# Preparing a state-space scan by batch pair, and moving 19 of its products to GpSimd

## The reference, cut to what matters

```python
x = einsum('bld,ed->bel', ctx, in_proj_w); x = silu(conv1d(x, conv_w) + conv_b)     # u, 256 channels
dt_low, Bm, Cm = split(einsum('bdl,ed->bel', x, x_proj_w), [8, 24])                  # 8 + 16 + 16 rows
dt = softplus(einsum('brl,dr->bdl', dt_low, dt_proj_w) + dt_proj_b)                  # delta
def step(state, inp):                                                                # 256 time steps
    state = state * exp(dt * A) + (dt * u) * B                                       # 16 states a channel
    return state, einsum('bdn,bn->bd', state, C)
y = (y + D * u) * silu(layernorm(x))                                                 # then x = x + y
```

## Time and profile before

| what | value |
|---|---|
| median of 3 runs | 987.07 us (983.51 to 987.46) |
| the profiled execution's own time | 985.21 us |
| its span | 983.4 us |
| mean granted clock of PE | 0.912 |
| busy PE, DVE, ACT, POOL | 82%, 75%, 47%, 25% |

### The profile page before, as it was taken

How to read it: one execution, slowest core, us unless ns; L and a number is a source line. 1 busy time by engine, 2 the same in 40 slices (tenths; PEclk the granted TensorE clock), 3 DMA queues, 4 the chain that set the end, 5 groups by cost and what they waited for, 6 DMA issues and landing times.

```text
span 983.4 us, 11811 instructions
## 1 busy us (share of the span) xinstructions
PE 806.8 (82%) x3952; PEld 577.3 (59%) x3952; DVE 741.3 (75%) x1080; ACT 459.3 (47%) x951; POOL 243.4 (25%) x162
## 2 busy tenths in 40 slices
PE   6822549997788996698998987988984789999997
PEld 3312435555533473466665665656763579999996
DVE  4599899999987897789899788869956744434443
ACT  1422445563114302467666656646773434544542
POOL 1072200000223012101011021111002447666663
PEclk9765658998899999899999999999997799999999
DMA  4222133221502022011111111011200034433431
GB/s 158 91 95 84 44 107 107 107 86 65 203 2 90 22 86 86 3 46 40 63 44 44 44 44 43 23 43 43 88 1 0 1 128 156 149 139 129 157 129 43
DMA packets 24176, 74.60 MB, mean 76 GB/s; under 512 B 3088, under 2 KB 5664, under 8 KB 23744
## 3 DMA queue, kind: packets, MB, share of 16 engines
q1 hardware_dynamic: 23776, 71.51, 20.7%
q10 hardware_dynamic: 352, 2.49, 0.8%
HBM read 72.55 MB, written 1.44 MB: 75 GB/s over the span
## 4 chain that ended last, share of the span: by engine, by line
PE 46%; DVE 30%; issue 11%; ACT 8%; POOL 2%; DMA 0%; POOLq 0%; DVEq 0%; SPq 0%; ACTq 0%
DVE hS L846 10%; PE ps L1457 6%; PE ps L1571 6%; PE ps L1572 6%; PE ps L1573 6%; DVE hS L838 4%; PE ps L1420 4%; PE ps L1536 3%; PE ps L1437 2%; PE ps L1524 2%; PE ps L1222 2%; PE ps L1230 2%; DVE arena L1097 2%; ACT dA L509 1%; PE ps L1515 1%
## 5 line engine op out<-in xcount | busy, mean ns | idle before, releaser
L846 DVE TENSOR_TENSOR_SCAN hS<-dA,hS 128x1024 f32<-128x1024 f32 x64 | 157.8, 2465 | 21.7 <-ACT dA L509 20.5
L1230 PE MATMUL ps<-ident,hS 128*128 128x128 f32 x512 | 75.8, 299 | 49.6 <-DVE hS L849 49.4
L1203 DVE SCALAR_TENSOR_TENSOR arena<-ps,arena 128x1024 f32<-128x1024 f32 x32 | 39.2, 1225 | 102.0 <-ACT arena L724 93.1
L1230 PEld LDWEIGHTS ps<-ident,hS 128*128 128x128 f32 x512 | 64.2, 154 | 77.7 <-DVE hS L849 59.3
L1457 PE MATMUL ps<-WB,hT 128*128 128x512 f32 x192 | 88.7, 606 | 3.8 <-DVE arena L1078 2.0
L509 ACT ACTIVATE dA<-DEL,negA 128x510 f32<-128x510 f32 x128 | 84.8, 717 | 12.3 <-DVE hS L846 11.8
L423 POOL TENSOR_TENSOR MHl<-arena,MHh 128x1024 fp32r<-128x1024 f32 x34 | 81.7, 2404 | 16.7 <-ACT MHh L727 16.7
L849 DVE TENSOR_TENSOR hS<-hS,BCb 128x1024 f32<-128x1024 f32 x64 | 83.6, 1306 | 2.2
L1571 PE MATMUL ps<-Wh,MHh 128*128 128x256 f32 x272 | 77.8, 286 | 6.0 <-POOL MHl L423 6.0
L409 POOL TENSOR_SCALAR jst<-jst 128x8 f32<-128x8 f32 x20 | 12.3, 613 | 279.6 <-DVE jst L1086 279.6
L838 DVE TENSOR_TENSOR hS<-DU,BCb 128x1024 f32<-128x1024 f32 x64 | 77.8, 1216 | 0.1
(11 more groups left out here) (206 smaller groups left out, 1889.5 us busy)
## 6 DMA issues: line engine op xcount, KB each, us to landing
BCb<-bc_dram SPq DMA_DIRECT2D x64, 512.0 KB, 3.6
arena<-gate_dram SPq DMA_DIRECT2D x32, 512.0 KB, 3.7
WB<-in_we SPq DMA_DIRECT2D x34, 256.0 KB, 2.7
WB<-in_wqkv SPq DMA_DIRECT2D x1, 3072.0 KB, 12.9
WA<-in_wo ACTq DMA_DIRECT2D x1, 2048.0 KB, 7.7
WA<-in_ffn SPq DMA_DIRECT2D x1, 1408.0 KB, 6.5
pkb<-in_pk SPq DMA_DIRECT2D x2, 698.0 KB
X<-in_x SPq DMA_DIRECT2D x1, 1024.0 KB, 7.4
```

The lines of the kernel that those rows point to most:

```text
L846: v.tensor_tensor_scan(f(h), f(a), f(h), 0.0, ALU.mult, ALU.add).then_inc(s["scan_done"], 1)
L1230: last = mm(ps[:, ACC_BANK + j // 2, 256 * (j % 2) + P * d:256 * (j % 2) + P * d + P], src[:, d, P * j:P * j + P], ident[:], start=(first ...
```

## The change

1. The preparation is done for each pair of the batch alone (k = 0, 1 in layer 0, k = 2, 3 in layer 1), with instructions of half the length. In layer 0 pair 0 is prepared first and half steps 0 to 2 run ahead of the rest of pair 1's preparation. Of the preparation, `d_u` moves from DVE to ACT, and for k above 0 so do `u_half`, max(z,0) (a Relu) and the addition of 1.
2. DVE's list in the head is reordered: half steps 3 to 5, then the rotary mean, 6 and 7, then the norm. PE adds half steps 0 to 7 ahead of the attention's transposes (0 to 3 before); ACT copies the projections after the exponentials of half step 2, and makes those of half steps up to 9 before it waits for `rope0_done` (up to 5 before).
3. `POOL_STEPS = range(8, 27)`: for half steps 8 to 26 of the first layer the C product moves to GpSimd, and the B product is written to PSUM banks 4 and 5, from which the scan reads it. The attention's PSUM banks shrink for it: scores have banks 0 and 1 alone, values bank 2, transposes bank 3, and `s0(u)` waits for tanh(u-1).
4. SP loads X ahead of two small tensors, and the second layer's weights after `delta_ready` 2.

```diff
+POOL_STEPS = range(8, 27)
+        def temps(k):
+            if k == 1:
+                two = lambda a: a.rearrange("p (d t) -> p d t", d=DT)
+                return (two(ar(38, 1024)), two(ar(42, 1024)), two(WB[:, 0, 2048:3072]), ar(46, 512)[0:DR + 2 * DS, :])
+            i = k % 2
+            return (ring(hS, 2 * i), ring(hS, 2 * i + 1), ring(dA, 2 + i), ring(dA, i)[0:DR + 2 * DS, 0, :])
@@ GpSimd, behind rope0_done
+            def times_c(g):
+                pool.wait_ge(s["scan_done"], g + 1)
+                pool.wait_ge(ld_bc[g % SB_LOADS], 16 * (g // SB_LOADS + 1))
+                h = ring(hS, g)
+                gp.tensor_tensor(h, h, BCb[g % SB_LOADS][:, 1:2, :].broadcast_to([P, DT, HALF]), ALU.mult).then_inc(s["c_ready"], 1)
+            for g in POOL_STEPS:
+                times_c(g)
@@ ACT
+            def softplus(k):
+                act.wait_ge(s["dtpre_mm"], k + 1)
...
+                for d in range(DT):
+                    sc.activation(DEL[:, d, pair(pr)], ps[:, CONV_BANK[l] + 2 * pr + d, :], ACT.Relu,
+                                  bias=pk[l][:, PK_DB + d:PK_DB + d + 1]).then_inc(s["sp_max"], 1)
+                act.wait_ge(s["sp_exp"], k + 1)
+                sc.activation(one, e, ACT.Identity, bias=1.0).then_inc(s["sp_one"], 1)
...
             neg_a(0)
             for d in range(DT):
                 conv_tanh(0, d)
-            ln_tr_copy(0)
+            conv_tanh(1, 0)
             xdbl_copy(0)
             softplus(0)
             softplus_ln(0)
-            for t in range(NT):
-                act.wait_ge(s["qkv0_mm"], t + 1)
-                sc.copy(Q0[:, t, :], ps[:, 4 + t % 4, 0:NQKV0]).then_inc(s["qkv0_copied"], 1)
+            conv_tanh(1, 1)
+            for d in range(DT):
+                u_half(1, d)
+            ln_tr_copy(0)
...
+            steps_to(0)
+            d_u(0)
+            xdbl_copy(1)
+            steps_to(1)
+            softplus(1)
+            softplus_ln(1)
             steps_to(2)
+            for t in range(NT):
+                act.wait_ge(s["qkv0_mm"], t + 1)
+                sc.copy(Q0[:, t, :], ps[:, 4 + t % 4, 0:NQKV0]).then_inc(s["qkv0_copied"], 1)
@@ DVE
+            def dbu(g):
+                return ps[:, DBU_BANK:DBU_BANK + 2, :] if g in POOL_STEPS else ring(hS, g)
...
-                v.tensor_tensor(ring(hS, g), DU[:, :, pair(pr)], b, ALU.mult).then_inc(s["dbu_ready"], 1)
+                if g in POOL_STEPS:
+                    dve.wait_ge(s["scan_done"], g)
+                    dve.wait_ge(s["qkv0_copied"], NT)
+                v.tensor_tensor(dbu(g), DU[:, :, pair(pr)], b, ALU.mult).then_inc(s["dbu_ready"], 1)
...
-                v.tensor_tensor_scan(f(h), f(a), f(h), 0.0, ALU.mult, ALU.add).then_inc(s["scan_done"], 1)
+                v.tensor_tensor_scan(f(h), f(a), f(dbu(g)), 0.0, ALU.mult, ALU.add).then_inc(s["scan_done"], 1)
+                if g in POOL_STEPS:
+                    return
                 dve.wait_ge(s["scan_done"], g + 1)
+                if g == POOL_STEPS.stop:
+                    dve.wait_ge(s["c_ready"], g)
...
-            for g in range(4, LAYER_STEPS - 4):
+            for g in range(8, LAYER_STEPS - 4):
                 ssm_step(g)
                 for u in range(UNITS0):
                     if AT0_AT[u] == g:
                         at0(u)
@@ PE
+            conv(1, (0,))
+            xdbl(0)
+            dtpre(0)
+            conv(1, (1,))
             pe.wait_ge(ld["ident"], 16)
             ln_tr(0)
-            xdbl(0)
+            xdbl(1)
+            dtpre(1)
             pe.wait_ge(ld["wqkv0"], 16)
-            dtpre(0)
...
-            for g in range(4):
+            for g in range(8):
                 acc(g)
             pe.wait_ge(s["rope0_done"], 1)
...
-                if u >= 2:
-                    pe.wait_ge(s["s0_tanh"], u - 1)
+                if u:
+                    pe.wait_ge(s["s0_tanh"], u)
```

More of the change, by code:

```diff
@@ L263, in build @@
         CONV_BANK = [0, 4]
+        DBU_BANK = 4
         ACC_BANK = 6
@@ L293, in _ @@
                 load_bc(g)
-            sp.wait_ge(s["delta_ready"], 1)
-            sp.wait_ge(s["sp_exp"], 1)
+            for g in range(SB_LOADS, 8):
+                load_bc(g)
+            sp.wait_ge(s["delta_ready"], 2)
+            sp.wait_ge(s["sp_exp"], 2)
             sp.wait_ge(s["nega_exp"], 1)
@@ L302, in _ @@
             sp.dma_start(dsc[:], io["dsc"]).then_inc(ld["ffn"], 16)
-            for g in range(SB_LOADS, LAYER_STEPS):
+            for g in range(8, LAYER_STEPS):
                 load_bc(g)
@@ L600, in _ @@
             neg_a(1)
-            for d in range(DT):
-                conv_tanh(1, d)
+            for k in (2, 3):
+                for d in range(DT):
+                    conv_tanh(k, d)
+                for d in range(DT):
+                    u_half(k, d)
             ln_tr_copy(1)
@@ new lines, in u_calc, with delta_max0 @@
+            def u_calc(k, d, mark=None):
+                l, pr = prep(k)
+                if k == 0:
+                    ch.wait(mark)
+                else:
+                    dve.wait_ge(s["conv_tanh"], DT * k + d + 1)
+                    dve.wait_ge(s["u_half"], DT * (k - 1) + d + 1)
+                v.scalar_tensor_tensor(U[:, d, pair(pr)], DEL[:, d, pair(pr)], 1.0, DU[:, d, pair(pr)], ALU.add,
+                                       ALU.mult).then_inc(s["u_ready"], 1)
+            def delta_max0():
+                for d in range(DT):
+                    dve.wait_ge(s["sp_abs"], d + 1)
+                    ch.step(v.tensor_scalar(DEL[:, d, pair(0)], ps[:, CONV_BANK[0] + d, :], pk[0][:, PK_DB + d:PK_DB + d + 1], 0.0,
+                                            ALU.add, ALU.max))
@@ L898, in _ @@
                 ln_stats(0, hf)
+            for d in range(DT):
+                u_calc(0, d, u_half0(d))
             for hf in both:
                 ln_apply(0, hf)
-            for d in range(DT):
-                u_calc(0, d, u_half(0, d))
-            for hf in both:
-                ln_tr_copy(0, hf)
-            delta_max(0)
+            delta_max0()
             delta_round(0)
@@ L909, in _ @@
             ssm_dbu(0)
-            d_u(0)
+            for hf in both:
+                ln_tr_copy(0, hf)
+            for d in range(DT):
+                u_calc(1, d)
+            ssm_scan(0)
+            ssm_step(1)
+            ssm_step(2)
+            delta_round(1)
+            delta_sum(1)
+            delta_u(1)
             dve.wait_ge(s["qkv0_copied"], NT)
@@ L996, in _ @@
                 ln_tr_copy(1, hf)
-            marks = [u_half(1, d) for d in range(DT)]
-            for d in range(DT):
-                u_calc(1, d, marks[d])
+            for k in (2, 3):
+                for d in range(DT):
+                    u_calc(k, d)
             dve.wait_ge(ld["ffn"], 48)
```

267 lines of the change are left out of this document (149 added, 118 removed).

## The result

The changed kernel takes **992.24 us** (median of 7 runs, 989.90 to 993.62) beside 986.74 us for the kernel before on the same chip (982.50 to 988.82): a ratio of 1.0077, 95% interval 1.0049 to 1.0104. 981.5 us was forecast, with a range to 991. The profiled execution of after took 993.62 us, its span 991.8.

A forecast was written before the change was run, and what follows sets the result against it. DVE was taken to bound the head, with PE almost level (5.08 against 5.14 us) in unit half steps. 985.2 - 2.7 - 1.9 = 980.6, or 982.5 from the median; 981.5 was taken, own range 977 to 987, with rivals 972 to 991.

The forecast's parts named there:

- DVE starts 0.03 us later, GpSimd 0.08 us later, so DVE is first: Half steps without at0: after a scan, DVE's B product gets the port before GpSimd's C product.
- the 3.57: Forecast length in us of a half step without at0, 1.22 + 2.29 + 0.06, against 4.72 before.
- the forecast's own case: The main forecast, no rival coming true: 981.5 us, own range 977 to 987, chance 0.58.
- The mid transpose: Around scan(20) to scan(22): PE's chain from at0(8) to at0(9) stays 8.54 us; gives back 2.5 us.
- PE's clock falls in the unit steps: Rival, attention-unit half steps: idle PE drops to 1.2 GHz, some 3.5 us per iteration; 992 to 1002 us, chance 0.08.
- The head: Start through scan(13): B(0) 20 us earlier, rope0_done at 120.4, scan(13) at 147.4 against 156.6; gain 9.2 us.
- The loop: Half steps with at0: GpSimd holds up the B product, 5.78 us against 5.14, 9.0 us lost over 14 intervals.
- p: Time of one C product on GpSimd: taken as 2.3 us, range 2.2 to 2.4.
- The C product can't be won in the unit half steps: Half steps with attention units: PE would stop the C product's 1.2 us gain after 0.06 us a step.
- Layer 1's preparation: Layer 1 up to hid(11): PE's 2.75 us stall goes, hid(11) at 338.8 instead of 340.7; -1.9 us.
- The port rival: Half steps with units: GpSimd doesn't hold the B product, PE bounds at 5.08 us; 974 us, chance 0.18.
- 980.6: Forecast sum in us for the whole kernel: 985.2 (profiled execution) - 2.7 - 1.9.

The follow-up runs named there:

- e7: Changed kernel with one added wait: GpSimd's C product of a half step waits for DVE's next B product; 973.44 us.
- e2: Changed kernel with the B product's wait for the scan put last and its wait for the copied projections made only at half step 8; 991.91 us.
- e5: On top of e2, the B product's waits for its BCb load and PE's sum moved ahead of the scan; 987.16 us.
- e1: Changed kernel with POOL_STEPS empty: no C product on GpSimd, no B product in PSUM, preparation by pair kept; 981.28 us.
- e4: Changed kernel with only the first half of each GpSimd C product, the other half left out; 971.67 us in one run.
- e9: e7 with C products on GpSimd only in half steps 8 to 12, those without at0; 978.06 us.
- e6: The order of e3 (next B product ahead of at0), but every C product on DVE and every B product in SBUF; 977.67 us.
- e8: e7 with the B product of half step 27 written to PSUM too; 973.35 us.
- e3: On top of e2, the wait of e7 and the next B product issued ahead of at0 on DVE; 974.17 us.

## Why the prediction was wrong

- **The step that failed: "DVE starts 0.03 us later, GpSimd 0.08 us later, so DVE is first".** The 0.03 us was that of DVE instructions with one wait in front, such as the C products; the new B product has four, and starts 0.20 us behind the scan. The race for the port in half steps 11 and 12 was lost by a tenth of a microsecond, and each lost half step cost 2.3 us (5.84 against 3.57): 4.5 of the 8.65 us by which scan(27) came late. Of these the race itself is 11.67 - 7.51 = 4.2 (e7 has B first, with the same four waits), and 0.3 are the start delay, which the 3.57 had left out. e2 and e5 show the cause: start delays of 0.20, 0.13 and 0.04 us as waits are reordered and taken from between, and GpSimd's 0.08 in the middle of them. I had given this comparison no rival and no chance, although it hung on 0.05 us. That is also why the range missed: the loss belongs to the forecast's own case, and without its 4.2 us the time would be 988.0, inside the range.
- **The mid transpose (mis-sized).** 8.54 us from the end of at0(8) to the start of at0(9) were taken over from before; it took 205.16 - 195.06 = 10.10. The difference is the clock in three rows: transposes 1.97 against 1.09 us, values 3.60 against 3.28, the sum 1.46 against 1.09, together 1.57. It isn't the slower loop: e1, whose loop is before's, took 197.94 - 187.95 = 9.99. The new preparation brings PE to this place ahead of DVE and idle (3.94 us in e1, 5.34 in after, 0.89 before), so 1.4 us of what it gained in the head is lost here. The cause stood in the forecast as a rival for the whole stage ("PE's clock falls in the unit steps"), with iterations of 5.08 us in mind and not this one place. The rival as it was put didn't come: by the view of its line the 56 matmuls of the values take 592 ns in the median and 1061 at most, and the window's clock is 0.92. One dip there was among the unit steps: the values at 160.51 took 2.90 us (granted clock 0.66 from 160 to 164), and the interval was 5.83 all the same, where the rival had priced 3.5 us.
- **The head (term too small by 1.8 us).** rope0_done came 1.2 us later than drawn and scan(10) another 0.6. Its lead, its 6.9 us wait for dA(2) and its order were right; e1 shows it by itself. Part of this varies with nothing edited: pair 1's dt projection took 3.78 us in the traces of after, e1, e2 and e7 and 1.98 in the six others, and scan(10) ends between 134.22 and 136.35 in them.
- **The loop (right).** 5.84 us against 5.78, p 2.35 against 2.3; e4 confirms the formula with p halved. That this would lose against 5.14 was the core of the forecast, and it did: 4.9 us in 13 to 20, 3.6 in 22 to 27.
- **The C product can't be won in the unit half steps (right, but not the whole).** e7 gains nothing there, yet e9 shows 2.9 us at the transpose that only come with it.
- **Layer 1's preparation.** From scan(27) to hid(11) it was 108.29 us before and 107.39 after: 0.9 gained, 1.9 forecast. In e4, e5 and e6, with the same preparation, it was 106.2 to 106.3, so the gain is 0.9 or 2.0 by the moment at which PE's clock rises (see e8); that after's trace missed the forecast by 1.0 is no more than that. PE's stall of 2.75 us went, and smaller ones came:

```profile
323.22 3.67 PE L1523 MATMUL ps<-hT,WA 128*128 128x512 f32 x8 [0.50 <-DVE arena L1130]
328.53 14.60 PE L1523 MATMUL ps<-hT,WA 128*128 128x512 f32 x32 [1.64 <-DVE arena L1130]
```

- **The port rival** (the port doesn't hold the B product in the unit steps) didn't come either: every B product that meets a GpSimd product is held. Its time, 974, is what e7 reaches in another way, by keeping the two apart.

The sum once more: 980.6 + 8.65 (up to scan(27)) + 1.0 (up to hid(11)) = 990.3, against a profiled execution of 993.62 whose untouched stages took 3.4 us longer than those of before.

## What to carry to other kernels

When two engines are released by the same event and only one of them can have the port, don't leave the order to start delays: they are tenths of a microsecond and change with the waits in front of an instruction. A wait of the one for the other's instruction costs nothing where the loser has slack, and here it turned a loss of 5.5 us into a gain of 13.4, of which 5.3 are the preparation's. And where PE is the bound and the lane engines only just keep up, read what PE does at its longest pause: freeing them may shorten no loop and still pay there, through the clock.

## What was not expected of the hardware

- **Start delay.** In all these kernels it goes with the count of waits written in front of a DVE instruction that the one before it releases: one or two, 0.03 to 0.04 us (C products; B in e5; the scan in after); three, 0.13 (B in e2 and e3); four, 0.20 (B in after and e7; the scan in e5). Whether the count or the place of the wait that ends last decides, and why, isn't shown. GpSimd started 0.08 us behind the same event. The Trainium skill, "SBUF — State Buffer", section "Who interferes with whom", says that a DVE instruction with two SBUF inputs contends with a GpSimd instruction that reads SBUF, and that the order of issue, not the shape of the operation, decides who blocks. The traces agree: the record that is long is the later one's, 3.31 us on DVE in after and 3.41 on GpSimd in e5, with the same two instructions; and here 0.05 us decided between them.
- **The loser's end.** Held by GpSimd, a B product ended 1.08 to 1.10 us behind it, whether GpSimd's took 1.26 or 2.35 us: 0.12 to 0.14 less than its own 1.22.
- **PSUM input and output.** A scan with one input in PSUM took 2.29 us, as with both in SBUF; a B product into PSUM took 1.22 to 1.23. The 62 extra cycles that the Trainium skill, "VectorE: DVE Perf Modes", section on the TRN2 errata, gives a PSUM source, left out of the prediction's sum, don't show in these records.
- **Independent work between dependent instructions.** A scan starts 1.26 us behind the start of the B product that it reads; an instruction that doesn't read it starts 1.13 behind. Putting at0 between the two hides the difference: 5.01 us a half step instead of 5.13 (e6 against e1).
